# A planner's due times: later query and key products, and naturals placed within six tenths of a unit

## The chip, the cores and the metric

The kernel runs on one core of one Trainium2 chip. The metric is the time on the device in microseconds (us). Every engine of the core (TensorE or PE, VectorE or DVE, ScalarE or ACT, GpSimd or POOL, and SP, which only issues transfers) works through a queue of its own in order and meets the others at semaphores.

## What is computed

```python
x  = L0_attn_x                                   # (2, 1024, 256), float32
xn = layernorm(x)
q, k, v = (einsum('btc,hcd->bhtd', xn, W) + b)   # 16 heads of 16
probs = softmax(q @ k.T * 16**-0.5 + causal)
attn  = (probs @ v) reshaped @ Wo + bo
logits = xn @ Wr ; two best of 8 experts per row, softmax over the two
ffn = sum over e: w_e * ((clip(silu(xn @ Wg[e]), -7, 7) * (xn @ Wu[e])) @ Wd[e])
out = x + attn + ffn
```

## The kernel before

The order of everything is set before the kernel is built. `make_plan` declares jobs with an engine, a length, what they come after and a due time; `Planner.run` then lays them out one by one: of all jobs that are open it takes the one that can start soonest, and among equals the one with the earliest due time. A PSUM bank is a resource in this, with at most three naturals, three scores and two query or key products in banks at once (`ROOM`), and TensorE jobs of another kind than the last have their due time put 8000 ns later (`STAY`), since changes of kind have a price (`SWITCH`). What comes out is one list of stages for each engine, and each engine's block walks its list. The planner's lengths are its own; the chip only gets the order.

The stages, by name in the code and line in the profile:

- **Products.** `qk1` and `qk2` (L1140) are the two halves of one of 16 products of 512 rows with query or key weights; `hi` (L820) and `mid` (L826) on ScalarE, `resid` (L921) on VectorE and `lo` (L746) on POOL split each into three bfloat16 parts; SP stores a pair (`store`, L650) and loads them as packed rows (`load`, L663) for a unit. ScalarE's `hi` waits for the landing of the store two pairs back. Products 0 to 3 and 4 to 7 are the first batch row (units 0, 1 and units 2, 3). `v` (L1164) makes values and router logits for 128 rows.
- **Attention** goes in eight units of four heads. Of a unit there are first the **naturals** (`nat`, L1209): 48 chunks of scores with rows on partitions, 16 early and 32 late, whose row maxima VectorE takes (`max`, L949 on the diagonal, L952 elsewhere). `negate` (L961 to L969) turns them into bfloat16 parts, TensorE transposes these (`neg`, L1215), VectorE copies (L976), and SP writes the rows into the packed queries (L673). Then come the **scores** in 12 steps (`s`, L1228), which contain the maximum already, the exponential on ScalarE (`exp`, L848), a mask on POOL on the diagonal (L786), and the weighing of v (`pv`, L1247). Unit 0 has two such copies: neg 0 (early maxima, for steps 0 to 3) and neg 1 (for steps 4 to 11). `y_t` (L1255), `norm` (L982, L987), `proj_t` (L1264) and `proj` (L1273) close a unit.
- **Router and experts.** VectorE finds the two best experts (`top`, L1014, `topi`, L1020), makes one-hot tables (`hot`, L1031), places rows (L1037 to L1054) and builds row tables (`rows`, L1060) and digit tables (`tiles`, L1067 to L1070); TensorE counts (`route`, L1172 to L1179) and writes the lists (`list`, L1190). Only then can POOL gather rows (L760) and fetch weights (L772) for 39 tiles of 128 rows; a tile is a transpose (L1280), gate and up (L1290), tanh (L876) and hid (L1107, L1110), down (L1299), and a scatter (L778). The row tables lie in the memory of the attention's output `y`, so the first `norm` comes behind the list. The results are summed with the projection at the end (L997, L999, L1008).

The due times that matter here: attention's steps are spread from 60 to 425 us (`due_at`), a unit's naturals over the first `SPREAD` of the unit ahead of it (`nat_due`), and products 4 to 15 from 15 us on, 1.5 us apart.

Of the kernel before, what the change touches and what calls it, by code (L numbers as in the profile page):

```python
# [48 lines left out]
UNITS = B * G  # L49
# [12 lines left out]
NS = len(STEPS)  # L62
# [173 lines left out]
          ("c", "b"): 110, ("c", "f"): 120}  # L236
STAY = 8000
NEG_LAG = 8000
SPREAD = 0.75
RATE = 280  # L240
SMALL = 65536
WARM = 60
# [3 lines left out]
def make_plan():  # L246
# [3 lines left out]
    def pe(stage, ns, after=(), due=0, takes=None, mode="f", lag=None):  # L250
# [5 lines left out]
    due_at = [a0 + (a1 - a0) * (u * sum(weight) + sum(weight[:n])) / (UNITS * sum(weight))  # L256
              for u in range(UNITS) for n in range(NS)] + [a1]
    nat_weight = [chunk_width(m) + 150 for m in range(NCH)]

    def nat_due(u, m):  # L260
        if u == 0:
            return 5000 if m < EARLY else 30000 + 400 * (m - EARLY)
        begin, end = due_at[NS * (u - 1)], due_at[NS * u]
        return begin + (end - begin) * SPREAD * sum(nat_weight[:m]) / sum(nat_weight)

    for n, (ns, due) in enumerate(((1100, -30), (2000, 30), (1800, 31))):
# [13 lines left out]
    for k in range(QKS):  # L280
        b, grp, op, n = qk_tile(k)
        w = k // 2
        due = 10 * n + 6 + op if k < 4 else 15000 + 1500 * (k - 4)
        after = [("ACT", ("xnt", 2 * b + n, c)) for c in range(DC)] + [("ACT", ("weights",))]
        pe(("qk1", k), 853, after, due=due, takes=("qk", k))
        pe(("qk2", k), 853, [("PE", ("qk1", k))], due=due - 1)
        job("ACT", ("hi", k), 570, [("PE", ("qk2", k))] + ([("SP", ("store", w - 2))] if w >= 2 else []), due=due)
        job("DVE", ("resid", k), 662, [("ACT", ("hi", k))] + ([("POOL", ("lo", k - 2))] if k >= 2 else []), due=due,
            frees=("qk", k))
        job("ACT", ("mid", k), 524, [("DVE", ("resid", k))], due=due)  # L290
        job("POOL", ("lo", k), 1175, [("ACT", ("mid", k))], due=due)
        if op:
            job("SP", ("store", w), 1500, [("POOL", ("lo", k))], due=due, lag=2000, size=786432)

    for t in range(NT):
        due = 10000 + 600 * t
        pe(("v", t), 884, [("ACT", ("xnt", t // 4, c)) for c in range(DC)] + ([("DVE", ("v_ones",))] if t == 0 else []),
           due=due, takes=("v", t))
# [26 lines left out]
    for u in range(UNITS):  # L325
        b, g = divmod(u, G)
        for c in range(2):
# [3 lines left out]
            due = 8 + 10 * c if u == 0 else 60000 + c if u == 1 else nat_due(u, 0) - 30000 + c  # L331
# [3 lines left out]
    for u in range(UNITS):  # L335
        for m in range(NCH):
            width, due = chunk_width(m), nat_due(u, m)
# [3 lines left out]
    for x, (u, c0, c1) in enumerate(NEGS):  # L341
        due = nat_due(u, 0)
# [6 lines left out]
    for g in range(NS * UNITS):  # L349
        u, n = divmod(g, NS)  # L350
        c, j = STEPS[n]
        due, width = due_at[g], step_span(n)[1]
# [14 lines left out]
        if last_of_half(n):  # L367
            due = due_at[g + 1]
# [20 lines left out]
    for i in range(MAX_TILES):  # L389
        due = m0 + (m1 - m0) * i / MAX_TILES  # L390
# [965 lines left out]
```

How the kernel before makes its waits and increments, by code:

```python
        def wait_room(pe, stage):  # L597
            bank, n = FILL_AT[stage]
            if n:
                pe.wait_ge(freed[bank], n)
            return bank, filled[bank]
# [1 line left out]
        def wait_filled(eng, stage):  # L604
            bank, n = FILL_AT[stage]
            eng.wait_ge(filled[bank], n + 1)
            return bank
# [1 line left out]
        def wait_freed(eng, stage):  # L609
            bank, n = FILL_AT[stage]
            eng.wait_ge(freed[bank], n + 1)
# [1 line left out]
        def wait_weighed(eng, g):  # L614
            u, n = divmod(g, NS)
            if last_of_half(n):
                wait_filled(eng, ("y", u, STEPS[n][0]))
            else:
                eng.wait_ge(pv_done, pv_counted(g))
# [17 lines left out]
            def spread_ones():  # L638
                sp.wait_ge(consts, 2)
                sp.dma_start(packk[MAXROW:KROWS, :, :, :, :].rearrange("p s c h t -> p (s c h t)")
                             .rearrange("p (r t) -> p r t", t=T),
                             ones_row[MAXROW:KROWS, :].unsqueeze(1).to_broadcast([PARTS, SLOTS * UH, T])).then_inc(ones_in, 16)
# [1 line left out]
            def store(w):  # L644
                b, grp, _, n = qk_tile(2 * w)
                sp.wait_ge(qk_lo, 2 * w + 2)
                for part in range(PARTS):
                    cols = slice(T * b + BANK * n, T * b + BANK * (n + 1))
                    sp.dma_start(qk_d[:, grp, part, :, :, cols].rearrange("o d h t -> (d h) o t"),
                                 stage[:, w % 2, part, :].rearrange("p (o t) -> p o t", o=2)).then_inc(qk_out[w % 2], 16)
```

## Time and profile before

| | us |
|---|---|
| median of three runs (lowest, highest) | 471.8 (470.96, 472.11) |
| the profiled execution, its own time | 466.59 |
| its span, first to last instruction | 464.8 |
| TensorE busy / VectorE busy / ScalarE busy | 429.5 / 313.4 / 243.8 |
| mean granted TensorE clock, of full speed | 0.978 |

The span and every row below are of the profiled execution. A clock of 1.00 in a stretch is 2.4 GHz throughout; the lower level is 1.2 GHz, so 0.75 is half of the stretch at either. TensorE's matmuls are pipelined and their ends are modelled, so starts are the better measure. A wait is the idle time of an engine ahead of an instruction, named by who released it.

### The profile page before, as it was taken

What the parts mean: (1) busy time and instruction counts of PE and PEld (TensorE: products, weight loads), DVE (VectorE), ACT (ScalarE), POOL (GpSimd) and SP (SyncE); (2) the same over time, 40 slices, a digit from 0 to 9 for tenths busy, and PEclk for the clock granted to TensorE, in tenths of its full rate; (3) what the DMA queues carried; (4) which work ended last, traced back from release to release, by engine and by line L of the source; (5) the groups of instructions that cost most, each with busy time, mean ns of one, the idle gap of its engine ahead of it and who ended that gap; (6) DMA issues with size and microseconds to landing.
All of it is one profiled execution on the core that took longest, in us unless ns stands there. A gap on an engine that the chain in (4) does not pass through costs nothing.

```text
span 464.8 us, 8495 instructions
## 1 busy us (share of the span) xinstructions
PE 429.5 (92%) x2851; PEld 253.5 (55%) x2851; DVE 313.4 (67%) x1007; ACT 243.8 (52%) x607; POOL 196.3 (42%) x239
## 2 busy tenths in 40 slices
PE   7999969479989999999999979999999999999985
PEld 7585423133563465556575656566564665557434
DVE  4917797998987847756747555765767665672593
ACT  1564355026438646644645536655566554655862
POOL 5411225141353375456843554246633654324211
PEclk9999979968999999999999999999999999999999
DMA  8089884236392269353944388144955444400691
GB/s 277 13 211 261 240 219 135 69 118 246 66 190 77 80 161 252 97 176 104 253 169 148 102 212 243 37 147 135 249 153 168 115 171 132 128 21 21 203 298 45
DMA packets 40374, 71.35 MB, mean 154 GB/s; under 512 B 5893, under 2 KB 30598, under 8 KB 40332
## 3 DMA queue, kind: packets, MB, share of 16 engines
q0 software_dynamic: 9360, 39.99, 26.9%
q1 hardware_dynamic: 27996, 27.54, 24.3%
q10 hardware_dynamic: 2976, 3.29, 2.2%
q8 instruction: 23, 0.38, 0.4%
q14 instruction: 19, 0.16, 0.1%
HBM read 55.85 MB, written 15.60 MB: 154 GB/s over the span
## 4 chain that ended last, share of the span: by engine, by line
PE 74%; DVE 7%; DMA 6%; ACT 5%; issue 4%; POOL 2%; SPq 1%; another core or an unknown queue 0%; ACTq 0%; POOLq 0%
PE psum L1247 14%; PE psum L1290 14%; PE psum L1228 13%; PE psum L1209 12%; PE psum L1299 8%; PE psum L1140 4%; DMA qk_parts<-stage 3%; ACT probs L848 3%; PE psum L1273 3%; DVE psum L949 2%; PE psum L1164 2%; PE psum L1280 2%; DMA x<-in_x 2%; DVE mxa L952 2%; PE psum L1255 1%
## 5 line engine op out<-in xcount | busy, mean ns | idle before, releaser
L848 ACT ACTIVATE probs<-psum 128x512 f32<-128x512 f32 (+3 forms) x384 | 158.6, 508 | 60.8 <-PE psum L1228 54.8
L949 DVE CUSTOM_DVE_ANT_0 psum<-psum,maskrow 128x128 f32<-128x128 f32 (+3 forms) x256 | 122.2, 505 | 30.7 <-PE psum L1209 27.5
L1228 PE MATMUL psum<-packq,packk 99*128 99x512 bf16 (+3 forms) x384 | 98.3, 335 | 4.7 <-ACT probs L848 3.1
L1209 PE MATMUL psum<-packk,packq 96*128 96x512 bf16 (+3 forms) x384 | 96.5, 334 | 4.4 <-ACT probs L848 1.6
L952 DVE TENSOR_REDUCE mxa<-psum 128x1 f32<-128x512 f32 x128 | 87.8, 686 | 11.6 <-PE psum L1209 11.2
L1247 PE MATMUL psum<-probs,v 128*32 128x512 f32 (+3 forms) x768 | 77.5, 495 | 3.9 <-POOL probs L786 3.2
L786 POOL TENSOR_SCALAR_AFFINE_SELECT probs<-probs 128x512 f32<-128x512 f32 x64 | 41.2, 647 | 78.1 <-ACT probs L848 76.2
L1209 PEld LDWEIGHTS psum<-packk,packq 96*128 96x128 bf16 x384 | 35.5, 99 | 55.4 <-issue 18.6
L1228 PEld LDWEIGHTS psum<-packq,packk 99*128 99x128 bf16 x384 | 35.0, 98 | 52.2 <-issue 18.0
L760 POOL DMA_INDIRECT xg<-xn_rows,token x39 | 37.7, 967 | 34.4 <-PE psum L1280 27.3
L1107 DVE SCALAR_TENSOR_TENSOR tanh<-tanh,psum 128x256 f32<-128x256 f32 x39 | 16.4, 420 | 49.9 <-ACT tanh L876 40.8
L778 POOL DMA_INDIRECT expert_rows<-yo,slots x39 | 39.4, 1011 | 23.4 <-issue 12.6
L1290 PEld LDWEIGHTS psum<-xgt,wexp 128*128 128x128 f32 x384 | 45.2, 192 | 3.9 <-issue 3.4
L1290 PE MATMUL psum<-xgt,wexp 128*128 128x128 f32 x384 | 46.9, 276 | 0.0
L876 ACT ACTIVATE tanh<-psum 128x256 f32<-128x256 f32 x39 | 15.0, 384 | 60.4 <-PE psum L1290 56.1
L772 POOL DMA_INDIRECT wexp<-in_wexp,wrow x24 | 23.2, 968 | 54.4 <-PE psum L1299 37.5
L746 POOL TENSOR_TENSOR stage<-resid,stage 128x512 bf16<-128x512 f32 x16 | 19.8, 1254 | 30.7 <-ACT stage L826 30.6
L1140 PE MATMUL psum<-xnt,wqk 128*128 128x512 f32 x64 | 32.1, 626 | 0.7 <-DVE resid L921 0.7
L1247 PEld LDWEIGHTS psum<-probs,v 128*32 128x32 f32 x768 | 17.2, 108 | 27.9 <-issue 20.5
L882 ACT ACTIVATE yo<-psum 128x256 f32<-128x256 f32 x39 | 15.0, 386 | 28.7 <-PE psum L1299 27.8
L1290 PEld LDWEIGHTS psum<-xgt,xnt 128*128 128x128 f32 x240 | 28.8, 192 | 1.6 <-issue 1.1
L1290 PE MATMUL psum<-xgt,xnt 128*128 128x128 f32 x240 | 29.5, 276 | 0.0
(121 smaller groups left out, 470.2 us busy)
## 6 DMA issues: line engine op xcount, KB each, us to landing
qk_parts<-stage SPq DMA_DIRECT2D x24, 256.0 KB, 3.2
stage<-expert_rows SPq DMA_DIRECT2D x16, 256.0 KB, 4.0
packq<-qk_parts SPq DMA_DIRECT2D x16, 192.0 KB
packk<-qk_parts SPq DMA_DIRECT2D x16, 192.0 KB
x<-in_x SPq DMA_DIRECT2D x4, 512.0 KB, 8.6
packq<-qk_parts SPq DMA_DIRECT2D x16, 128.0 KB
packk<-qk_parts SPq DMA_DIRECT2D x16, 128.0 KB
xn_rows<-probs ACTq DMA_DIRECT2D x4, 512.0 KB, 12.9
```

Of the source, the lines that this page charges most:

```text
L760: pool.indirect_dma_start(out=xg[:, i % 2, :], out_offset=None, in_=xn_d, in_offset=bass.IndirectOffsetOnAxis(ap=token[:, i:i + 1], axis=0))\
L778: pool.indirect_dma_start(out=z_d, out_offset=bass.IndirectOffsetOnAxis(ap=slots[:, i:i + 1], axis=0), in_=yo[:, i % 2, :], in_offset=None ...
L786: pool.affine_select(out=cols, in_=cols, compare_op=ALU.is_ge, fill=0.0, base=0, pattern=[[0, UH], [1, P]], channel_multiplier=-1).then_in ...
L848: act.activation(probs[:, g % RING, h, 0:width], psum[:, bank, 0:width], ACT.Exp, scale=SCALE)\
L949: ins = dve.tensor_tensor_reduce(out=chunk, in0=chunk, in1=maskrow[:, BANK - width:], scale=1.0, scalar=NEG, op0=ALU.add, op1=ALU.max, acc ...
L952: ins = dve.tensor_reduce(into, chunk, op=ALU.max, axis=AX.X)
L1140: return pe.matmul(psum[:, bank, :], wqk[:, op, c, P * grp:P * (grp + 1)], xnt_moe[:, c, cols], start=c == 0, stop=c == DC - 1)
L1209: pe.matmul(psum[:, bank, 0:width], packq[0:MAXROW, u % SLOTS, i // HALF, h, P * (i % HALF):P * (i % HALF + 1)], packk[0:MAXROW, u % SLOTS ...
L1228: pe.matmul(psum[:, bank, 0:width], packk[0:KROWS, u % SLOTS, j // HALF, h, P * (j % HALF):P * (j % HALF + 1)], packq[0:KROWS, u % SLOTS, ...
L1247: ins = pe.matmul(psum[32 * h:32 * h + 32, bank, t0 - BANK * c:BANK], v[:, TB * b + j, at:at + 32], probs[:, g % RING, h, 0:width], start= ...
L1290: ins = pe.matmul(psum[:, bank, P * m:P * (m + 1)], wexp[i % WSLOTS][:, at:at + P], xgt[:, i % 2, c, :], start=c == 0, stop=c == DC - 1)
L1299: ins = pe.matmul(psum[:, bank, 0:D], hid[:, i % 2, P * c:P * (c + 1)], wexp[i % WSLOTS][:, at:at + D], start=c == 0, stop=c == DC - 1)
```

## The change

Three numbers of the plan change: the due time of products 4 to 15, `SPREAD`, and, for the last unit alone, the time in which its naturals are due, which lies 10 us sooner.

```diff
--- before.py
+++ after.py
@@ -236,7 +236,7 @@
           ("c", "b"): 110, ("c", "f"): 120}
 STAY = 8000
 NEG_LAG = 8000
-SPREAD = 0.75
+SPREAD = 0.6
 RATE = 280
 SMALL = 65536
 WARM = 60
@@ -260,7 +260,8 @@
     def nat_due(u, m):
         if u == 0:
             return 5000 if m < EARLY else 30000 + 400 * (m - EARLY)
-        begin, end = due_at[NS * (u - 1)], due_at[NS * u]
+        ahead = 10000 * (u == UNITS - 1)
+        begin, end = due_at[NS * (u - 1)] - ahead, due_at[NS * u] - ahead
         return begin + (end - begin) * SPREAD * sum(nat_weight[:m]) / sum(nat_weight)
 
     for n, (ns, due) in enumerate(((1100, -30), (2000, 30), (1800, 31))):
@@ -280,7 +281,7 @@
     for k in range(QKS):
         b, grp, op, n = qk_tile(k)
         w = k // 2
-        due = 10 * n + 6 + op if k < 4 else 15000 + 1500 * (k - 4)
+        due = 10 * n + 6 + op if k < 4 else 35000 + 1500 * (k - 4)
         after = [("ACT", ("xnt", 2 * b + n, c)) for c in range(DC)] + [("ACT", ("weights",))]
         pe(("qk1", k), 853, after, due=due, takes=("qk", k))
         pe(("qk2", k), 853, [("PE", ("qk1", k))], due=due - 1)
```

Everything else in the order follows from the planner. The lengths of all lists of stages stay the same. On VectorE, at the copy of neg 1 (L976 before, L977 after; line numbers behind the change are one higher), the engine that is waited for there. `mxa` and `mxb` are row maxima, `negm` and `negr` their negated parts, `y` and `wexp` hold the router's tables, `topi` the indices of the best experts. Before:

```order
L949 ISA psum,mxa<-psum,maskrow 128x128
L949 ISA mxa 128x1
L961 TENSOR_TENSOR mxa<-mxa,mxb 128x16
L966 TENSOR_SCALAR negm<-mxa 128x16
L967 SCALAR_TENSOR_TENSOR negr<-mxa,negm 128x16
L968 CAST negm<-negr 128x16
L969 TENSOR_TENSOR negm<-negr,negm 128x16
L1060 TENSOR_TENSOR y<-iota_row,posrow 128x2048
L976 COPY negt<-psum 96x128
L1067 TENSOR_TENSOR wexp<-iota_t,postile 128x16x39
L1069 TENSOR_TENSOR wexp<-wexp,high_digit 128x16x39
```

The copy stands behind the second row table and in front of the second digit table. After:

```order
L922 SCALAR_TENSOR_TENSOR resid<-psum,bqk,stage 128x512
L962 TENSOR_TENSOR mxa<-mxa,mxb 128x16
L967 TENSOR_SCALAR negm<-mxa 128x16
L968 SCALAR_TENSOR_TENSOR negr<-mxa,negm 128x16
L969 CAST negm<-negr 128x16
L970 TENSOR_TENSOR negm<-negr,negm 128x16
L950 ISA psum,mxa<-psum,maskrow 128x128
L950 ISA mxa 128x1
L1021 MAX_INDEX topi<-top,lg 128x8 x16
L1022 TENSOR_TENSOR dl<-top 128x16
L977 COPY negt<-psum 96x128
```

The copy now stands ahead of both pairs of tables, of placing and of the one-hot table, with the residual of product 9 just ahead of the negation, and the index search in front of it.

On TensorE, ahead of the lists (L1190, L1191), the engine that waits there; `packk,packq` are naturals, `packq,packk` scores, `probs,v` the weighing, `ident,yraw` a transposition. Before:

```order
L1209 MATMUL psum<-packk,packq 128x256
L1209 MATMUL psum<-packk,packq 128x512
L1209 MATMUL psum<-packk,packq 128x384
L1209 MATMUL psum<-packk,packq 128x512 x2
L1209 MATMUL psum<-packk,packq 128x128
L1209 MATMUL psum<-packk,packq 128x256
L1209 MATMUL psum<-packk,packq 128x384
L1209 MATMUL psum<-packk,packq 128x512
L1215 MATMUL psum<-identb,negm 96x128
L1209 MATMUL psum<-packk,packq 128x128
L1190 MATMUL psum<-wexp,y 128x78 x32
```

Only naturals, of units 0 and 1, stand between the first transposition of the output and the lists. After:

```order
L1229 MATMUL psum<-packq,packk 128x128 x3
L1229 MATMUL psum<-packq,packk 128x512 x3
L1248 MATMUL psum<-probs,v 32x256 x4
L1229 MATMUL psum<-packq,packk 128x512
L1248 MATMUL psum<-probs,v 32x128 x4
L1229 MATMUL psum<-packq,packk 128x512 x2
L1256 MATMUL psum<-ident,yraw 128x128 x4
L1229 MATMUL psum<-packq,packk 128x512 x6
L1248 MATMUL psum<-probs,v 32x512 x12
L1229 MATMUL psum<-packq,packk 128x512
L1191 MATMUL psum<-wexp,y 128x78 x32
```

In this place stand unit 0's scores of steps 3 to 7 and their weighing of v; no natural is among them. The naturals of unit 1 from the ninth on come behind the lists.

Counted over the whole list, TensorE changes its kind of matmul 239 times before and 273 times after, 56 and 95 of them ahead of unit 1's first scores. Ahead of those stand, before, three gate and up products, two down products, three row transposes and 18 naturals of unit 2; after, six, four, six and 24. Unit 7's last 32 naturals stand within 26.0 us of TensorE work before and 19.0 after (each stage at its duration in the trace).

## Rows read from the trace of the kernel before

**Rows 1.** The page: busy time of TensorE and VectorE, chain by engine, weighing of v
```profile
PE 429.5 (92%) x2851; PEld 253.5 (55%) x2851; DVE 313.4 (67%) x1007; ACT 243.8 (52%) x607; POOL 196.3 (42%) x239
...
PE 74%; DVE 7%; DMA 6%; ACT 5%; issue 4%; POOL 2%; SPq 1%; another core or an unknown queue 0%; ACTq 0%; POOLq 0%
...
L1247 PE MATMUL psum<-probs,v 128*32 128x512 f32 (+3 forms) x768 | 77.5, 495 | 3.9 <-POOL probs L786 3.2
```

**Rows 2.** Busy by stretch; columns as the first line names them
```profile
core 0: us, PE busy (x) PEld busy (x) DVE busy (x) ACT busy (x) POOL busy (x), PEclk, DMA share, GB/s
46.00:137.00 91.00, 74.29 (x420) 35.02 (x421) 78.93 (x277) 35.83 (x78) 30.41 (x31) 0.89 0.60 160
46.00:60.00 14.00, 11.67 (x33) 5.07 (x33) 10.92 (x72) 4.43 (x9) 4.59 (x4) 1.00 0.89 239
80.00:95.00 15.00, 6.53 (x49) 3.04 (x50) 14.52 (x42) 2.32 (x8) 3.50 (x4) 0.86 0.20 64
95.00:110.00 15.00, 13.80 (x77) 5.89 (x74) 13.46 (x51) 6.73 (x12) 6.87 (x7) 0.68 0.65 214
137.00:428.00 291.00, 283.77 (x2022) 173.33 (x2020) 187.06 (x590) 165.04 (x418) 143.79 (x167) 1.00 0.49 144
428.00:465.00 37.00, 30.21 (x211) 15.02 (x211) 20.22 (x46) 22.66 (x59) 6.36 (x9) 1.00 0.53 171
```

**Rows 3.** The chain that ended last: start us, us, what
```profile
26.88 5.34 PE psum L1164 x24
...
90.31 2.28 DVE y L1060
...
99.58 0.59 DVE psum L949
...
124.33 5.50 DMA xg<-xn_rows,token
...
133.68 1.79 PE psum L1290 x16
```

**Rows 4.** Timeline of VectorE: start us, us, engine, line, operation
```profile
46.82 0.21 DVE L976 COPY negt<-psum 96x128 bf16<-96x128 bf16 x1
...
48.16 0.09 DVE L1020 MATCH_VALUE_LOAD topi<-top,lg 128x8 f32 x1
...
50.47 0.75 DVE L921 SCALAR_TENSOR_TENSOR resid<-psum,bqk,stage 128x512 f32<-128x512 f32 x1
...
61.67 0.28 DVE L1037 TENSOR_TENSOR fits<-psum,iota 128x128 f32<-128x128 f32 x1
...
64.54 1.41 DVE L921 SCALAR_TENSOR_TENSOR resid<-psum,bqk,stage 128x512 f32<-128x512 f32 x2
...
85.11 0.69 DVE L952 TENSOR_REDUCE mxa<-psum 128x1 f32<-128x512 f32 x1
...
89.14 0.33 DVE L949 CUSTOM_DVE_ANT_0 psum<-psum,maskrow 128x128 f32<-128x128 f32 x1
...
92.52 0.21 DVE L976 COPY negt<-psum 96x128 bf16<-96x128 bf16 x1
...
92.65 0.80 DVE L1067 TENSOR_TENSOR wexp<-iota_t,postile 128x624 bf16<-128x624 f32 x1
...
94.50 0.43 DVE L949 CUSTOM_DVE_ANT_0 psum<-psum,maskrow 128x256 f32<-128x256 f32 x1
```

**Rows 5.** Timeline of TensorE, three places
```profile
36.44 0.76 PE L1209 MATMUL psum<-packk,packq 96*128 96x128 bf16 x5
...
94.69 2.24 PE L1190 MATMUL psum<-wexp,y 128*128 128x78 bf16 x32 [3.93 <-issue]
...
136.99 1.03 PE L1228 MATMUL psum<-packq,packk 99*128 99x512 bf16 x4
```

**Rows 6.** Timelines of SP's queue and ScalarE
```profile
43.06 1.46 SPq L650 DMA_DIRECT2D qk_parts<-stage  x3
...
54.08 0.69 ACT L820 ACTIVATE stage<-psum,bqk 128x512 bf16<-128x512 f32 x1 [3.31 <-DMA qk_parts<-stage]
...
56.78 3.94 SPq L650 DMA_DIRECT2D qk_parts<-stage  x6
...
62.70 1.27 ACT L820 ACTIVATE stage<-psum,bqk 128x512 bf16<-128x512 f32 x2 [4.68 <-DMA qk_parts<-stage]
...
92.75 1.77 SPq L673 DMA_DIRECT2D packq<-negt  x3
```

## The prediction

> **What bounds the kernel now.** I read the page's first table and its chain of waits first. TensorE (PE) is busy 92% of the span and carries 74% of the chain that ended last; VectorE (DVE) stands at 67% [rows 1]. So the end moves when TensorE's idle time, or its time at the lower clock, changes: the change leaves every matmul in place. Next I read the table by stretch, to see where those two lie. From 137 to 428 us TensorE is busy 283.8 of 291 us at full clock, 7.2 us idle. From 428 on it is idle about 6.6 us of 36.8, in the drain of the last unit. But from 46 to 137 us it is idle 91 - 74.3 = 16.7 us, at a mean granted clock of 0.89, so about 20 us of that stretch ran at 1.2 instead of 2.4 GHz [rows 2]. This early stretch is the pool from which the change can gain. Within it, from 80 to 95 us, TensorE works 6.5 of 15 us while VectorE works 14.5: VectorE is the engine that ends last there.
>
> The chain of waits says the same: from 84 to 100 us it runs over VectorE (row maxima, then the one-hot tables of the router), and later over one gather of expert rows [rows 3]. In order of time, VectorE copies the first unit's early maxima at 46.8 us (neg 0), then does the whole top-two search, residuals and router tables; it finishes unit 0's later maxima, 32 chunks, only at about 89.4 us and copies neg 1 at 92.5, after the first half of the router's second table [rows 4]. The scores of the second half of unit 0 need that copy on its way through SP (issued 92.75), so they start near 100 us; the routing list is on TensorE at 94.7; unit 1's first scores run at 137.0 [rows 5, 6]. TensorE had nothing else: its queue is in order, and what stands there is unit 1's naturals, which wait for VectorE.
>
> **The change part by part.** No operation is added or taken out, so the direct price is zero; all of it is order.
>
> (1) Query and key products 4 to 15 come later. Until 36 us nothing starves: v products fill the place (5.34 us for six [rows 3], 0.89 each, which the copy on ScalarE keeps up with), and naturals begin near 36.4 us as now [rows 5]. Unit 0's naturals now run straight through: in the order, all 48 stand ahead of product 10. The two stores to DRAM that these products feed come later on SP, behind neg 0, and with them unit 2's loads; unit 2's naturals stand far behind the lists, so this is hidden. What it costs if that cover is gone: the next products wait for the landing of a store two pairs back. Rows show 11.0 us for one (issued 43.06, released ScalarE at 54.08), among heavy traffic, and 5.9 us for the next (56.78 to 62.70); I take 6, since the loads that crowded the queue at 43 us are gone by then, and keep 11 in the range [rows 6].
>
> (2) VectorE from 46.8 us. A head of eight late chunks takes 85.11 to 89.14 = 4.03 us, four heads 16.1 [rows 4]. In the new order, behind the copy of neg 0, there stand about 31 of these chunks (15.6 us), six residuals at 0.67 (0.75 less the overlap, 4.0), the negation (0.9: from the last chunk at 89.14 to the table at 90.31 [rows 3], less 0.25 for the chunk), one small chunk (0.2) and the index search (48.16 to 50.47 = 2.3). Sum 23.1: neg 1 is copied at 46.8 + 23.1 = **70 us instead of 92.5**. TensorE keeps up with that: up to neg 1 it has 12.2 (before its first real work) + 48.6 us of matmuls, 61 us, and waits about 8 for VectorE.
>
> (3) Then the router on VectorE: six residuals (4.0), seven small steps at 0.3 (2.1), four diagonal chunks (4.03 less four others at 0.6, which is 0.69 less the overlap: 1.6), placing (61.67 to 64.54 = 2.9), two row tables at 2.2 (4.4), two digit tables at 1.85 (92.65 to 94.50; 3.7). Sum 18.7, ready at 88.7 us. TensorE has 18.8 us of matmuls from neg 1 to the list: last products 6.9, weighing of v for seven steps 5.7 (0.81 each in the mean [rows 1]), scores 4.0, the rest 2.2; with 2 us of changes of kind (some 0.1 each), 70 + 21 = 91. The list, 2.2 us [rows 5], ends at **93 us, against 96.9**: the router itself gains 4 us at most. The gain is that scores and v of six and a half steps lie ahead of it, where TensorE stood idle.
>
> (4) From the list to neg 2: TensorE 22.5 us of matmuls (scores and v of steps 7 to 11, 40 naturals, four gate/up products) plus 2.7 us of changes; VectorE 1 + 40 chunks (19.7) + 1.4 + 1.2 = 23.3. The last four chunks are ahead of neg 2 on both, and naturals run at most three ahead of VectorE, so I add 2.5 for the coupling: 93 + 27.7 = 120.7. From there to unit 1's first scores 10.8 us of matmuls: 131.7. The experts' inputs: gather 2 stands on POOL behind the mask of step 11 in both orders and took 5.5 us to land [rows 3]; now it is issued near 108, lands near 114, and is wanted at 115. No gain, no loss; if late, up to 2 us.
>
> (5) The clock. My walk is at full clock. TensorE has pauses in 47 to 57 and again near 70 us, so it will lose some; before, about 10 us of half clock fell where TensorE was the bound (95 to 110: 0.68 [rows 2]). I take 2 us: **133.7 us against 137.0**, 3.3 sooner. And more is done by then: ahead of unit 1's first scores the new order has three more gate/up products (3 x 1.79 [rows 3]), two down products (1.7), three transposes (0.7) and six late naturals (1.1), 8.9 us. So TensorE is 3.3 + 8.9 = **12.2 us ahead**.
>
> (6) SPREAD and the last unit. From there on both orders hold the same work but 8.9 us less, with 5 fewer changes of kind (the planner's own price, 0.1 each; 0.5). Naturals come denser: of unit 7 the last 32 lie within 19.0 us of TensorE work and need 18.7 on VectorE, where now it is 26.0 to 19.7. That is the tightest place; -1 to +3 us, taken as +0.5. In the drain, the first eight heads' projection now stands ahead of step 6's scores, so ScalarE rests there and has four more exponentials behind it (2 us) while TensorE has 0.9 less ahead: even, 0 to 1.
>
> Sum: 464.8 - 12.2 = 452.6 us of span, 454.4 for the profiled execution (466.6 before, with 1.8 around the span). The median of the runs is 471.8, 5.2 above that execution; the difference is taken from it: **471.8 - 12.3 = 459.5 us**.
>
> **The rivals.** (A) *The gain is given back* in 137 to 428 us. Being ahead is worth something only while TensorE is the bound there. For: denser naturals make VectorE and TensorE wait for one another in units 5 to 7; 1.5 us for each of six units gives back 9. Against: idle 7.2 of 291 us [rows 2]. Time 468. By the Trainium skill, "Trainium Kernel Development and Optimization", Performance Expectations, matmul busy time says little of how near TensorE is to its limit and weight-load time says more; the page shows 55% for the latter. That rule would make this rival likely; the short waits in 137 to 428 speak against it.
>
> (B) *Only the router counts*: the experts' chain (39 tiles) sets the end, and it starts 4 us sooner: 468. Against: the end is paced by a full TensorE, and POOL, which issues their transfers, is little in the chain (2%) [rows 1]. A and B end alike.
>
> (C) *Slower: the clock.* In 47 to 57 us the order leaves TensorE small naturals with gaps, in place of long products. If the clock falls there and stays low until the list and beyond, each microsecond of bound TensorE work costs one more. Up to neg 2 some 43 us of work are concerned; from 14.2 us of it on, the gain is gone; 20 us give 471.8 - 14.2 + 20 = 477.6. For: after 92 us the clock stayed low for much of 15 us though TensorE was busy 13.8 of them [rows 2]. Against: in 46 to 60 it stayed full with 2.3 us idle. The Trainium skill, "TensorE: Matmul & The Clock Gate", section "Why this matters for your kernels", has it that pauses between bursts bring the throttle, which speaks against this order of short bursts; the trace agrees as far as the drops begin behind waits.
>
> (D) *It does nothing*: a store's landing (11 us, [rows 6]) holds products 12 to 15 and so the router, 6 us late, and the clock takes the rest: within 0.3%, 471.8.
>
> (E) *More*: no clock loss and tighter coupling, gain 18 to 20: 452.5.
>
> **How the numbers follow.** A measurement can tell about 0.3%, 1.4 us. Forecast (454 to 464) 0.58; A and B (464 to 470.3) 0.17; E 0.05; D 0.07; C 0.13. Faster 0.80, same 0.07, slower 0.13. The range takes in E's edge and A and B: 452.5 to 470.
>
> **What would show it.** Neg 1's copy near 70 and its SP issue at 70 to 72 us; VectorE busy nearly throughout 47 to 89; TensorE's list near 91; idle from 46 us to unit 1's first scores down from 16.7 to about 9, with those scores near 134; mean clock there 0.9 or more; some 8 us idle from there to the last down product. Wrong if: the clock is under 0.8 in 50 to 120 (C), ScalarE waits over 6 us for a store (D), or TensorE's idle time behind unit 1's first scores grows by more than 5 us (A).

## The result, and the profile after

The changed kernel runs in 467.98 us (median of 20 runs) beside 470.69 us for the kernel before on the same chip: 0.9941 of its time, 95% interval 0.9915 to 0.9968. That is faster by 0.6%, or 2.7 us, where 12.3 us was forecast: the sign is right, the size is not. The time lies inside the stated range (452.5 to 470), but outside the band given the most weight (454 to 464). Measured twice more, the ratio was 0.9979 (0.9949 to 1.0009) and 0.9993 (0.9957 to 1.0029); the mean of the three is 0.997, by which the gain is about 1.3 us (an estimate over three chips).

The profiled execution of the changed kernel took 467.66 us, its span is 465.9. That of before (466.59) lies under all 20 runs that the kernel before has beside the changed one (468.49 at the lowest), so the ends of the two traces say little.

The page after, for [rows 1]: busy times, chain by engine, weighing of v.

```profile
PE 434.4 (93%) x2851; PEld 257.6 (55%) x2851; DVE 315.0 (68%) x1007; ACT 243.8 (52%) x607; POOL 195.0 (42%) x239
...
PE 71%; DVE 16%; ACT 4%; DMA 3%; issue 3%; POOL 2%; another core or an unknown queue 1%; POOLq 0%; SPq 0%; DVEq 0%; ACTq 0%
...
L1248 PE MATMUL psum<-probs,v 128*32 128x512 f32 (+3 forms) x768 | 76.9, 496 | 4.6 <-POOL probs L787 3.9
```

The chain now runs over VectorE for 16% of the span (7% before). The table by stretch after, for [rows 2]; columns are the stretch, its length, busy us (and count) of PE, PEld, DVE, ACT, POOL, the granted clock, DMA share, GB/s.

```profile
46.00:137.00 91.00, 79.95 (x460) 39.84 (x461) 83.93 (x270) 40.43 (x87) 36.22 (x38) 0.94 0.60 168
46.00:60.00 14.00, 11.83 (x35) 4.76 (x36) 13.73 (x43) 3.23 (x5) 3.18 (x3) 0.88 0.34 110
80.00:95.00 15.00, 13.52 (x77) 4.86 (x79) 14.27 (x19) 11.00 (x26) 6.61 (x6) 0.95 0.32 106
95.00:110.00 15.00, 13.96 (x106) 4.88 (x98) 13.72 (x51) 8.00 (x19) 8.79 (x10) 1.00 0.61 214
120.00:130.00 10.00, 7.14 (x47) 6.56 (x47) 6.62 (x27) 1.30 (x4) 1.89 (x2) 0.83 0.25 61
137.00:428.00 291.00, 281.61 (x1972) 170.86 (x1970) 182.89 (x585) 160.61 (x408) 138.06 (x162) 0.99 0.49 140
```

Before, TensorE stood idle for long in one place. That hole is gone: from 80 to 95 us TensorE is busy 13.5 of 15 us, not 6.5, and from 95 to 110 it has the full clock, not 0.68. Two things are new. From 120 to 130 us there is a smaller hole with the clock at 0.83, and from 137 to 428 us TensorE is idle 9.4 us instead of 7.2, its clock no longer full.

The milestones, for [rows 4, 5]: VectorE's copy of neg 1, TensorE's list, and unit 1's first scores.

```profile
71.44 0.22 DVE L977 COPY negt<-psum 96x128 bf16<-96x128 bf16 x1
...
95.93 1.23 PE L1191 MATMUL psum<-wexp,y 128*128 128x78 bf16 x29
...
140.48 1.03 PE L1229 MATMUL psum<-packq,packk 99*128 99x512 bf16 x4
```

Neg 1 was forecast for 70 (92.5 before) and came at 71.4. The list was forecast for 91 and came at 95.9; neg 2 for 120.7, and came at 128.7; unit 1's scores for 133.7, and came at 140.5. With the 8.9 us of work moved ahead of them, TensorE is 8.9 - (140.5 - 137.0) = 5.4 us ahead there, not 12.2. The first scores of units 4 and 6, after and before:

```profile
270.73 1.04 PE L1229 MATMUL psum<-packq,packk 99*128 99x512 bf16 x4
378.97 0.38 PE L1229 MATMUL psum<-packq,packk 99*128 99x512 bf16 x1
```
```profile
280.49 0.81 PE L1228 MATMUL psum<-packq,packk 99*128 99x512 bf16 x3
377.90 1.03 PE L1228 MATMUL psum<-packq,packk 99*128 99x512 bf16 x4
```

The two orders have different amounts of work ahead of these places: at unit 4 the new one has 4.3 us less done, at unit 6 1.6 us more (estimates, each matmul at its usual spacing in the traces). So the lead is 9.8 - 4.3 = 5.5 us at unit 4, as at unit 1, and 1.6 - 1.1 = 0.5 us at unit 6. At unit 7's first scores (428.5 for 426.5) it is -1.9. Of the 7.4 us lost between units 4 and 7 about 3.4 are the lower clock (0.98 in the mean over 270.7 to 428.5, for 1.00) and 3.0 more idle time of TensorE (5.7 us there, 2.7 before).

**Where the list is late.** VectorE's router steps became slower. Its timeline after; the first number is the start, the second the duration.

```profile
67.58 1.02 DVE L968 SCALAR_TENSOR_TENSOR negr<-mxa,negm 128x16 f32<-128x16 f32 x1
...
87.27 1.07 DVE L1068 TENSOR_TENSOR wexp<-iota_t,postile 128x624 bf16<-128x624 f32 x1
88.38 1.65 DVE L1070 TENSOR_TENSOR wexp<-wexp,high_digit 128x624 bf16<-128x624 bf16 x1
89.94 1.28 DVE L1071 TENSOR_SCALAR wexp<-wexp,low_digit 128x624 bf16<-128x624 bf16 x1
...
93.34 0.80 DVE L1068 TENSOR_TENSOR wexp<-iota_t,postile 128x624 bf16<-128x624 f32 x1
94.18 0.81 DVE L1070 TENSOR_TENSOR wexp<-wexp,high_digit 128x624 bf16<-128x624 bf16 x1
94.90 0.39 DVE L1071 TENSOR_SCALAR wexp<-wexp,low_digit 128x624 bf16<-128x624 bf16 x1
```

The same three steps of a digit table take 4.0 us at 87 and 2.0 us at 93. What differs is GpSimd, which splits the products' third parts (`lo`) at just these times:

```profile
66.15 2.41 POOL L747 TENSOR_TENSOR stage<-resid,stage 128x512 bf16<-128x512 f32 x2 [0.67 <-ACT stage L827]
...
87.65 3.39 POOL L747 TENSOR_TENSOR stage<-resid,stage 128x512 bf16<-128x512 f32 x2
```

From 66 to 92 us, VectorE's instructions beside such a subtraction take 5.7 us more than their like without one, 1.4 of it ahead of neg 1 and 4.3 behind it; in before it is about 1.1 us, two instructions at 75 and 76 us, since there only two subtractions lay beside router steps. By the Trainium skill, "SBUF — State Buffer", section "Who interferes with whom", GpSimd and VectorE have a port pair in common that one of them holds for a whole instruction; the durations agree with that.

**Where neg 2 is late.** TensorE's timeline, with the wait ahead of an instruction in brackets:

```profile
119.72 0.38 PE L1281 MATMUL psum<-ident,xg 128*128 128x128 f32 x2
119.98 0.22 PE L1210 MATMUL psum<-packk,packq 96*128 96x128 bf16 x1
123.05 0.69 PE L1281 MATMUL psum<-ident,xg 128*128 128x128 f32 x2 [2.86 <-DMA xg<-xn_rows,token]
123.53 0.42 PE L1210 MATMUL psum<-packk,packq 96*128 96x256 bf16 x1
123.75 3.00 PE L1291 MATMUL psum<-xgt,wexp 128*128 128x128 f32 x16
```

The rows of tile 3 are not there. Their gather needs one of two buffers of `xg`, which the transposes of tile 1 free; on GpSimd, gathers 2 and 3:

```profile
112.28 0.95 POOL L761 DMA_INDIRECT xg<-xn_rows,token  x1 [0.99 <-PE psum L1281]
116.61 0.95 POOL L761 DMA_INDIRECT xg<-xn_rows,token  x1 [3.38 <-PE psum L1281]
```

The gather for tile 3 is issued at 116.6, and its rows are used at 123.1. Behind the wait the clock has fallen: 16 matmuls of gate and up take 3.00 us where they take 1.95 to 2.02 around it.

### The profile page after: what moved, and what is told of

Same layout as the page of the kernel before. It is cut to its first block, busy times and chain, and to the rows that moved or that the text cites. A ratio compares the mean times of both kernels' runs of the same rounds, so it can differ in the third digit from the quotient of the medians.

```text
span 465.9 us, 8495 instructions
## 1 busy us (share of the span) xinstructions
PE 434.4 (93%) x2851; PEld 257.6 (55%) x2851; DVE 315.0 (68%) x1007; ACT 243.8 (52%) x607; POOL 195.0 (42%) x239
## 3 DMA queue, kind: packets, MB, share of 16 engines
q1 hardware_dynamic: 27996, 27.54, 23.9%
## 4 chain that ended last, share of the span: by engine, by line
PE 71%; DVE 16%; ACT 4%; DMA 3%; issue 3%; POOL 2%; another core or an unknown queue 1%; POOLq 0%; SPq 0%; DVEq 0%; ACTq 0%
PE psum L1291 15%; PE psum L1248 13%; PE psum L1210 12%; PE psum L1229 10%; PE psum L1300 7%; DVE psum L950 5%; ACT probs L849 4%; PE psum L1274 3%; PE psum L1141 3%; DVE mxa L953 3%; PE psum L1165 3%; PE psum L1281 2%; DMA x<-in_x 2%; PE psum L1256 2%; DMA xg<-xn_rows,token 1%
## 5 line engine op out<-in xcount | busy, mean ns | idle before, releaser
L849 ACT ACTIVATE probs<-psum 128x512 f32<-128x512 f32 (+3 forms) x384 | 159.1, 513 | 50.6 <-PE psum L1229 48.0
L1229 PE MATMUL psum<-packq,packk 99*128 99x512 bf16 (+3 forms) x384 | 96.2, 329 | 4.5 <-issue 1.4
L953 DVE TENSOR_REDUCE mxa<-psum 128x1 f32<-128x512 f32 x128 | 87.9, 687 | 13.9 <-PE psum L1210 12.9
L1210 PEld LDWEIGHTS psum<-packk,packq 96*128 96x128 bf16 x384 | 35.3, 97 | 57.5 <-issue 23.1
L1291 PEld LDWEIGHTS psum<-xgt,wexp 128*128 128x128 f32 x384 | 48.4, 200 | 3.3 <-issue 2.1
L1291 PE MATMUL psum<-xgt,wexp 128*128 128x128 f32 x384 | 49.3, 284 | 0.3 <-DVE mxa L953 0.2
L1248 PEld LDWEIGHTS psum<-probs,v 128*32 128x32 f32 x768 | 18.4, 108 | 32.6 <-issue 22.8
L1141 PE MATMUL psum<-xnt,wqk 128*128 128x512 f32 x64 | 33.9, 645 | 1.1 <-DVE negt L977 0.7
```

Source lines behind the costliest of these rows:

```text
L849: act.activation(probs[:, g % RING, h, 0:width], psum[:, bank, 0:width], ACT.Exp, scale=SCALE)\
L953: ins = dve.tensor_reduce(into, chunk, op=ALU.max, axis=AX.X)
L1141: return pe.matmul(psum[:, bank, :], wqk[:, op, c, P * grp:P * (grp + 1)], xnt_moe[:, c, cols], start=c == 0, stop=c == DC - 1)
L1210: pe.matmul(psum[:, bank, 0:width], packq[0:MAXROW, u % SLOTS, i // HALF, h, P * (i % HALF):P * (i % HALF + 1)], packk[0:MAXROW, u % SLOTS ...
L1229: pe.matmul(psum[:, bank, 0:width], packk[0:KROWS, u % SLOTS, j // HALF, h, P * (j % HALF):P * (j % HALF + 1)], packq[0:KROWS, u % SLOTS, ...
L1248: ins = pe.matmul(psum[32 * h:32 * h + 32, bank, t0 - BANK * c:BANK], v[:, TB * b + j, at:at + 32], probs[:, g % RING, h, 0:width], start= ...
```

## The experiments

All ratios are to the kernel before on the same chip, with 95% intervals. The chips differ: before took 461.3 us on two of them and 468 to 471 on the others, so kernels are compared within a group of runs on one chip. Each kernel of this part was timed 12 times, but five of those with a third buffer only 6 times; their intervals are wider.

### Each edit alone

These four ran on one chip. **The kernel before again.** 

> The kernel before, unchanged, as a second trace and as a measure of what a repeat differs by. Every theory: ratio 1.000 within 0.003, some 470.7 us. If the profiled execution of before (466.6 us) was merely a quick one, this trace has the expert stage or the last unit some 2 to 4 us later than the first one had, with the same stages up to unit 1's first scores (near 137 us).

Measured: 1.0015 (0.9988 to 1.0042). In time this is 462.1 us, not 470.7: this chip is a faster one. Its trace has unit 1's first scores at 138.2, and is ahead of the first trace only from unit 4 on (first scores at 278.2 for 280.5, unit 6 at 374.2 for 377.9).

**Products alone**, one line:

```diff
-        due = 10 * n + 6 + op if k < 4 else 15000 + 1500 * (k - 4)
+        due = 10 * n + 6 + op if k < 4 else 35000 + 1500 * (k - 4)
```

> Only the due time of the products 4 to 15 is moved (35000 for 15000), the naturals keep 0.75 and the last unit's their place. Theory S (the products bring all of the gain, and it is carried to the end): the same as the changed kernel or better, ratio 0.990 to 0.995, 466 to 468 us. Theory G (the denser naturals give back in the units 4 to 6 what the start won, a lead of 5.4 us at unit 4's scores and 0.2 at unit 6's in the first pair of traces): without them the full 5.4 us is kept, ratio 0.988 to 0.990, some 465.3 us, 2 us and more below the changed kernel. Theory N (the naturals are what brings the gain): ratio 0.998 to 1.002, about 470.7 us.

Measured: 0.9963 (0.9937 to 0.9989), 1.7 us. This is clear of 1.000, but in no theory's range: the interval reaches into those of S and N, and G's (the full 5.4 us kept) falls. In its trace the list comes at 97.5 and unit 1's first scores at 144.4, behind waits for gathered rows (1.7 and 4.4 us) and half the clock from 125 on: the lead of the list is lost before unit 1.

**Spread alone** (`SPREAD = 0.6`). 

> Only the spread of the naturals goes from 0.75 to 0.6. The prediction priced this at about nothing: ratio 0.998 to 1.002. Theory G (denser naturals cost time in the units 4 to 6): 1.003 to 1.008, 472 to 474 us. Theory N (they bring the gain): 0.994 to 0.997, about 468.5 us.

Measured: 1.0061 (1.0024 to 1.0097), a cost of 2.8 us, as theory G expected. The forecast had it at about nothing. The profiled execution does not show that cost as a whole: its time is 462.8 us, for 463.9 of the kernel before on this chip.

**The last unit alone** (the two lines with `ahead`). 

> Only the last unit's naturals come 10 us of the plan's time sooner. The prediction gave this 0.5 us at the most: ratio 0.998 to 1.001. If it is the last unit's earlier naturals that crowd the units 5 and 6, 1.003 to 1.006 (472 to 473.5 us), with unit 6's first scores later than in before and the tail of unit 7 shorter by less.

Measured: 0.9989 (0.9954 to 1.0023), no difference that the interval can tell.

### What holds the start up

These four ran on one chip. **The changed kernel again.** 

> The changed kernel, unchanged, for a second trace and a second ratio against before. First ratio 0.994 (0.992 to 0.997). Every theory: 0.992 to 0.997. If the lead over before of 5.4 us at unit 4's first scores and 0.2 us at unit 6's, seen in the first pair of traces, is a property of the order (theory G), this trace shows again half a clock or idle time of TensorE between 300 and 380 us; if it was that one execution, this one keeps some 3 us of it or more.

Measured: 0.9979 (0.9949 to 1.0009), a little above the range of every theory. The second question is answered in part. Against the trace of before on the other fast chip the lead falls again, from 4.9 us at unit 4's first scores (269.0 for 278.2) to 2.1 at unit 6's (373.6 for 374.2) and -0.8 at unit 7's, which speaks for the order and against one odd execution; but between 300 and 380 us this trace has the full clock. At the start, the wait for tile 3's rows is larger here, and a smaller one stands before it:

```profile
120.32 0.44 PE L1281 MATMUL psum<-ident,xg 128*128 128x128 f32 x2 [0.89 <-DMA xg<-xn_rows,token]
120.59 0.22 PE L1210 MATMUL psum<-packk,packq 96*128 96x128 bf16 x1
125.26 0.69 PE L1281 MATMUL psum<-ident,xg 128*128 128x128 f32 x2 [4.44 <-DMA xg<-xn_rows,token]
125.74 0.42 PE L1210 MATMUL psum<-packk,packq 96*128 96x256 bf16 x1
125.95 3.62 PE L1291 MATMUL psum<-xgt,wexp 128*128 128x128 f32 x16
```

**Short subtractions on GpSimd**, in the changed kernel and in before. The kernel leaves out the third parts of 496 of 512 columns, and GpSimd sets their place to zero at the start (not shown here):

```diff
-                pool.tensor_tensor(stage[:, w % 2, stored(k, 2), cols], resid[:, k % 2, :], stage[:, w % 2, stored(k, 1), cols],
+                cols = slice(BANK * op, BANK * op + 16)
+                pool.tensor_tensor(stage[:, w % 2, stored(k, 2), cols], resid[:, k % 2, 0:16], stage[:, w % 2, stored(k, 1), cols],
```

> The changed kernel with GpSimd's subtraction for the third parts of queries and keys on 16 of the 512 columns (the other third parts are left at zero, so scores lose their last digits). Theory P (GpSimd's subtractions of 1.2 us each hold up VectorE's router steps, 5.7 us in the changed kernel's trace): the router's steps are back at their durations without a neighbour (hot 0.49 us and not 1.8), the token list 4 to 5 us sooner than in the changed kernel (91 to 92 us for 95.9), and the ratio to before 3 to 4 us lower than the changed kernel's, about 0.986 to 0.988. Theory Q (the list is late for another reason, the copies of ScalarE or a store): list within 1.5 us of 95.9, ratio 0.992 to 0.996.

> The same cut of GpSimd's subtractions in the kernel before, as the control. Theory P: two of them lie beside the router there, about 1 us of VectorE, and TensorE waits for negated maxima, not for the list: 0.997 to 1.000. If GpSimd's subtractions cost as much here as in the changed kernel (they hold up the chunk maxima or the stores as well), 0.990 to 0.993, and the cut tells nothing about the change.

Measured: the changed kernel 0.9988 (0.9952 to 1.0024), before 0.9964 (0.9934 to 0.9995). VectorE's slow steps are nearly gone (a digit table takes 2.0 us both times, the one-hot table 0.8 for 1.8), yet the changed kernel is no faster; before is, by 1.4 us, which is just below theory P's range for it and not in the other's. Two things in the trace of the changed kernel go with that. At the start, ScalarE's queue stands for 4.9 us at 36.8, in the issue of a store that takes 0.7 us in the changed kernel, and neg 1 comes at 74.5, 2.3 us later; that the zeros set by GpSimd cause this is not shown. The list comes 0.8 us later, so 1.5 us are won back up to there. And neg 2 stands at 132.1, with 132.2 in the changed kernel: TensorE's wait for the gathers takes up what was won. Theory P's mechanism held on VectorE; its price at the end did not. The test was not clean, and was made again below.

**A third buffer for gathered rows**, the order unchanged. The space is that of the query and key weights:

```diff
-        xg = sb("xg", [P, 2, D])
+        xg_own = sb("xg", [P, 2, D])
+        xg = [xg_own[:, 0, :], xg_own[:, 1, :], wqk[:, 0, 0, :]]
...
-                if i >= 2:
-                    wait_filled(pool, ("x", i - 2))
+                if i == 2:
+                    wait_filled(pool, ("qk", QKS - 1))
+                if i >= 3:
+                    wait_filled(pool, ("x", i - 3))
```

> The changed kernel with a third buffer for gathered rows (in the space of the query and key weights, free by then), so that gather 2 does not wait for the transposes of tile 0, nor gather 3 for those of tile 1. Everything is computed. Theory X (the gathers' chain, with the 2.9 us for which TensorE waits before the transposes of tile 3 and the half clock behind it, costs 3 to 4 us ahead of unit 1's first scores): no wait there, those scores at 136.5 to 138 us for 140.5, ratio to before 3 us lower than the changed kernel's, about 0.987. Theory Y (the wait only takes the place of one for neg 2, which VectorE could not have given sooner): scores of unit 1 within 1 us of 140.5, ratio 0.993 to 0.996.

Measured: 0.9893 (0.9847 to 0.9939), by the medians 4.6 us below before and 4.1 below the changed kernel on that chip. In its trace:

```profile
120.45 0.44 PE L1284 MATMUL psum<-ident,xg 128*128 128x128 f32 x2 [0.88 <-DMA xg<-xn_rows,token]
120.84 1.95 PE L1294 MATMUL psum<-xgt,wexp 128*128 128x128 f32 x16
123.01 1.95 PE L1294 MATMUL psum<-xgt,xnt 128*128 128x128 f32 x16
124.79 0.22 PE L1219 MATMUL psum<-identb,negm 128*96 128x128 bf16 x1
```

Tile 3 waits 0.9 us, not 4.4, the matmuls behind it have the full clock, neg 2 stands at 124.8 for 132.2, and unit 1's first scores at 136.2 for 143.3. Theory X holds; Y falls. Later traces agree: with the products moved and whole subtractions, unit 1's first scores stand at 140.5 to 144.4 us in the five traces with two buffers, and at 136.2 to 140.1 in the seven with three.

### Is it the change that needs the buffer?

Four more, on one chip. **Before with the third buffer.** 

> The kernel before with the third buffer for gathered rows; everything is computed. In its trace only one gather's wait shows on TensorE, 1.67 us at 129.88, and 1.7 us are all that can be won. Theory X1 (it is the change that puts the gathers on the path: work moved behind the list runs out before the rows come): 0.996 to 1.000 here, against the 0.989 of the changed kernel with the third buffer. Theory X2 (a third buffer is worth as much in either order, and the last run's gain says nothing on the change): 0.989 to 0.993.

Measured: 1.0035 (1.0000 to 1.0071), no gain; rather slower than X1's range. The wait of 1.67 us is gone from the trace, unit 1's first scores come 0.5 us sooner, and no gain is left at the end. X2 falls, and X1 is what remains: only the changed order gains from the buffer.

**Products alone, third buffer.** 

> Only the products' due time of the change, with the third buffer. Theory S (the products bring all of the gain; denser naturals and the last unit's lead bring nothing with the gathers free either): as the changed kernel with the third buffer, 0.987 to 0.992. If the denser naturals are what pays once the gathers do not hold TensorE up, 0.993 to 0.996. If they cost what they cost alone (1.006), 0.983 to 0.986 and the best kernel so far.

Measured: 0.9834 (0.9787 to 0.9882), 459.9 us for 467.8. This is what was expected if the denser naturals cost here what they cost alone, and the lowest ratio up to here.

**Short subtractions and third buffer**, the edit above from the fifth product on, so that the start stays. 

> The changed kernel with the third buffer, and GpSimd's subtraction for the third parts on 16 of 512 columns from the fifth product on (the first four whole, so that the start is as in the changed kernel; the other third parts keep what the first four left, so scores differ in their last digits). Theory P (5.7 us of VectorE's time beside those subtractions puts the list late, and with the gathers free that goes to the end): the list at 92 to 93 us for 95.8, unit 1's first scores at 133 us for 136.2, ratio 0.980 to 0.983. Theory R (VectorE ends 0.5 us before TensorE comes to the list; TensorE's own queue sets it): the list 1 to 2.5 us sooner at the most, ratio 0.985 to 0.989.

**The changed kernel with the third buffer, again.** 

> The changed kernel with the third buffer once more, since half of its runs were left out the first time. Every theory: 0.989 within 0.004, 4 to 6 us below before; its trace has unit 1's first scores at 136 to 137 us.

Measured: 0.9897 (0.9838 to 0.9956) with the short subtractions beside 0.9953 (0.9907 to 0.9998) without. The last is above the 0.985 to 0.993 that every theory expected, while its trace has unit 1's first scores where they were expected (136.4). Products alone is 7.5 us below it (459.9 for 467.4): what differs is the spread and the last unit. With the short subtractions the list stands at 92.0 for 95.6, unit 1's first scores at 134.6 for 136.4, the medians at 464.1 for 467.4. The ratio is above the ranges of both theories, its interval reaching into R's, and the two intervals overlap, so the 3.3 us at the end is a hint. The 3.6 us at the list is what theory P named; how they get there is more of theory R:

```profile
89.06 0.39 DVE L1076 TENSOR_SCALAR wexp<-wexp,low_digit 128x624 bf16<-128x624 bf16 x1
...
92.01 1.34 PE L1196 MATMUL psum<-wexp,y 128*128 128x78 bf16 x32
```

VectorE's last table is ready at 89.4, 5.5 us sooner, and 2.6 us ahead of the list, which stands where TensorE's own queue comes to it. Of the 3.6 us 1.8 are left at unit 1; between 115 and 125 us the granted clock is 0.83 there, a loss of 1.7 us, and 1.00 without the short subtractions.

### What the denser naturals cost

Four, on one chip, all with the third buffer: the two by two of the spread and the last unit.

> Products' due time and third buffer, once more, as the base of the two by two. Theory G (naturals give back): 0.983 to 0.987, the fastest of these four. Theory V (all four are equal, the earlier differences were of chips and runs): 0.988 to 0.992 for all four.

> The same with the spread at 0.6, the last unit's naturals where they were. Theory G, denser naturals are the cost (0.6% alone): 0.989 to 0.993, 3 us above the base. Theory V: as the base within 0.3%.

> The same with the spread at 0.75 and the last unit's naturals 10 us of the plan sooner. Alone that edit measured 0.999. Theory G by the spread: as the base within 0.3%, or 0.1% better. If it is the last unit's part that costs beside the moved products, 0.988 to 0.993.

> The changed kernel with the third buffer, all three edits, a third time (0.989 and 0.995 so far). Theory G: 0.990 to 0.995, 3 to 4 us above the base. Theory V: as the base within 0.3%.

| products moved, third buffer, and | runs | us | ratio (95%) |
|---|---|---|---|
| nothing else | 6 | 462.8 | 0.9813 (0.9768 to 0.9858) |
| spread 0.6 | 12 | 469.6 | 0.9994 (0.9961 to 1.0026) |
| last unit | 6 | 460.0 | 0.9776 (0.9735 to 0.9817) |
| both (the whole change) | 12 | 469.2 | 0.9954 (0.9921 to 0.9987) |

The spread takes 1.8% in the ratios, 6.8 us by the medians, nearly everything the products win (8.4 us); with the last unit's naturals sooner it takes 1.8% again, 9.1 us (460.0 to 469.2). Theory G names the direction; the cost is two to three times its 3 to 4 us. V falls. The last unit's edit costs nothing and may bring 0.4%; the intervals overlap. The kernel with the products moved, the last unit's naturals sooner and the third buffer, at the old spread, beats both: 0.9776, 11 us below before.

Why it costs, as far as the traces show. Two 20-us stretches at the end of unit 5's scores, first at spread 0.75, then at 0.6 (columns as above):

```profile
340.00:360.00 20.00, 19.92 (x129) 11.88 (x128) 13.79 (x40) 11.49 (x25) 7.94 (x9) 1.00 0.37 122
360.00:380.00 20.00, 19.43 (x154) 12.40 (x153) 11.52 (x43) 9.67 (x27) 12.40 (x15) 1.00 0.49 160
```
```profile
340.00:360.00 20.00, 19.34 (x121) 10.09 (x120) 16.61 (x51) 11.06 (x25) 6.78 (x8) 1.00 0.38 133
360.00:380.00 20.00, 17.88 (x119) 12.77 (x121) 5.44 (x19) 8.27 (x25) 10.31 (x12) 0.83 0.35 116
```

At 0.6 VectorE has more to do first (16.6 of 20 us), then almost nothing (5.4): most naturals are done, and TensorE has few left to put between the scores (6 of their matmuls from 360 to 380 us, for 15). It then stands still for short times, and what follows runs at half clock:

```profile
369.19 0.28 PE L1231 MATMUL psum<-packq,packk 99*128 99x128 bf16 x2 [0.53 <-issue]
...
370.77 0.38 PE L1231 MATMUL psum<-packq,packk 99*128 99x512 bf16 x1 [0.64 <-issue]
371.96 1.46 PE L1231 MATMUL psum<-packq,packk 99*128 99x512 bf16 x3 [0.82 <-ACT probs L851]
```

From unit 5's first scores to unit 6's it takes 50.6 us (320.2 to 370.8), against 46.0 (325.3 to 371.3) at 0.75; TensorE is idle 3.8 us of that, against 0.7, and has some 1 us more work. The lower clock comes behind it, in unit 6.

Between 145 and 430 us, the time lost to the lower clock is 0.0 us in all ten traces at spread 0.75, and 1.7 to 5.1 us in eight of nine at 0.6 with the products moved. From 430 us on it is the other way round: seven of the ten at 0.75 lose 1.8 to 3.4 us in the drain of the last unit, all at 0.6 at most 0.7. So the clock alone does not explain the cost; the idle time from 137 to 428 us is the other part (6.8 to 7.9 us with the third buffer at 0.75, and 5.9 to 12.6 at 0.6 and the products moved; 5.9 is the one trace on a fast chip).

With the spread alone the lower clock takes nothing behind 145 us. TensorE is idle 4.0 us from 137 to 428, for 2.4 in the trace of before on that chip: 1.6 of the 2.8 us. The rest I can't place.

### The same with two buffers

Two runs, on one chip: the change without its spread, and the whole.

> The change without its spread of 0.6: the products' due time and the last unit's naturals, two buffers for gathered rows. Theory G (the spread gives back what the products win): 0.985 to 0.992, 3 us and more below the changed kernel on this chip. Theory H (the two-buffer gathers cap the gain first, so that the spread makes no difference there): within 0.3% of the changed kernel, 0.993 to 0.998.

> The changed kernel, unchanged, on the same chip: 0.994 and 0.998 so far. Both theories: 0.993 to 0.998.

Measured: 0.9958 (0.9919 to 0.9997) and 0.9993 (0.9957 to 1.0029); medians 467.8 and 469.0. The second is a little above the range expected for it. The difference, 1.3 us, is less than the intervals can tell: G and H stay open here. The two traces tell more: at unit 7's first scores the kernel without the spread is far ahead (421.8 for 429.1; 5.4 us when the work done is counted), as G has it, and then gives most of it back. It loses 3.4 us to the lower clock in the drain (0.91 from 430 to 470, for 0.99), and the spans are 465.1 and 466.8. So in this pair of traces the spread costs time in units 4 to 6 with two buffers as well, and little of it reaches the end.

## Why the prediction was right or wrong

**Step 1, the products later: right.** Naturals start at 36.8. ScalarE waited 2.7 us for a store, once, at 77; rival D named over 6 us and falls.

**Step 2, neg 1 at 70: right** (71.4). From neg 0 to neg 1 VectorE took 23.9 us for 23.1 counted, though `mxa` and `negr` were 1.4 us slower beside GpSimd; the rest of the count was 0.6 us too long.

**Step 3, the router: mis-sized.** The forecast had VectorE ready at 88.7 and TensorE's queue at the list at 91; they came at 95.3 and 95.9. The sum took VectorE's durations from places where GpSimd did nothing. In the new order GpSimd's subtractions lie beside the router, and 5.7 us of VectorE's time goes to that, against 1.1 before. With the subtractions cut (and the third buffer) VectorE is ready at 89.4 and the list comes at 92.0: about 1 us from the forecast. By which waits VectorE's delay gets into TensorE's queue was not followed.

**Step 4, list to neg 2: mis-sized.** "Gather 2 stands on POOL behind the mask of step 11 ... no gain, no loss" looked at one gather and its queue. With two buffers each gather waits for the transposes of the tile two back. In the new order tiles 0 to 3 follow one another about 4 us apart on TensorE (111.6, 116.0, 119.7, 123.1; before, tile 3 comes only at 157.2), so gather 2 is issued at 112.3 instead of 108, and gather 3, of which nothing was said, at 116.6. Together with the lower clock behind the wait, list to neg 2 took 32.8 us for the 29.7 forecast, and 35.7 in the second trace. With the third buffer it takes 29.0. With both causes taken away, unit 1's first scores stand at 134.6; the forecast was 133.7 (and 0.2 less if its last sum is added rightly: 120.7 + 10.8 is 131.5).

**Step 5, the clock: about right, and not a fixed sum.** From 40 to 145 us the granted clock is 0.90 before and 0.95 or 0.93 after, so 10 us were lost to it before and 5 to 7 after, 3 with the third buffer. Before, after, after again and with the third buffer:

```profile
40.00:145.00 105.00, 87.56 (x488) 40.78 (x487) 90.53 (x317) 46.06 (x108) 36.80 (x39) 0.90 0.62 172
```
```profile
40.00:145.00 105.00, 93.06 (x522) 46.03 (x520) 97.86 (x329) 46.95 (x103) 43.13 (x45) 0.95 0.63 183
```
```profile
40.00:145.00 105.00, 90.88 (x513) 45.87 (x510) 95.16 (x320) 44.49 (x96) 40.99 (x41) 0.93 0.63 177
```
```profile
40.00:145.00 105.00, 95.12 (x563) 46.03 (x562) 99.51 (x332) 50.16 (x114) 45.94 (x49) 0.97 0.64 185
```

The forecast took 2 us for it and set them behind everything else. In the trace 5.1 are lost, in three dips of 1.7, near 51, 78 and 123 us. The first lies where TensorE waits for VectorE anyway; only the third lies behind the wait for the gathers, on the way to neg 2. Neg 2 came 8.0 us late (4.9 at the list, 3.1 from there on) and unit 1's scores 6.8: none of the clock's loss fell between the two, where the sum had put it. With the products alone, 10 us were lost again. TensorE's idle time from 46 to 137 us fell from 16.7 to 11.1 us; 9 was forecast. Rival C falls, since the dips are short and the mean clock is 0.94 from 46 to 137 us; so does B, since the list is later than before (95.9 for 94.7) and the 5.4 us ahead at unit 1 are work done; and so does E.

**Step 6, the spread: wrong.** It was taken at +0.5 us, by looking at the last unit alone. Alone it costs 2.8 us, and beside the moved products with the gathers free 6.8. With two buffers, as in the changed kernel, the times put it at 1.3 us and cannot tell that from nothing, though the traces lose their lead in units 4 to 6. This is rival A, in its place (units 5 to 7) and near its time (468); but only about half of the missing gain went its way, and the rest was lost ahead of unit 1, so that the time agrees is in part luck. A's own sign, over 5 us more idle time behind unit 1's first scores, did not show either: it was 2.2 us more (9.4 for 7.2), with 3.4 us of lower clock beside it, which A left out. A was argued against from the 7.2 us of idle time in 137 to 428 us of before. That argument failed: idle time there was short with the naturals mixed into the scores as they were, and says nothing of an order that puts them first. The last unit's edit was rightly priced (0 to 0.4% gain).

So of the 12.2 us ahead that were forecast, 6.8 were lost up to unit 1's first scores by steps 3 and 4, and the 5.4 left were lost in units 4 to 6, where the order of step 6 has the naturals early.

The kernel with the products moved, the last unit's naturals sooner and a third buffer gains 11.1 us, near the 12.3 of the forecast. That too is in part luck: its list comes at 96.2 and unit 1's first scores at 138.0, 5.2 and 4.3 us behind the forecast, like those of the changed kernel. In the changed kernel the gathers cap the gain at the start, and the spread takes what the buffer would give. The two do not add: by the medians the buffer with the spread kept gains 0.4 to 4.6 us on before (three chips), two buffers without the spread 3.1.

## What to carry to other kernels

- When a reorder brings the consumers of a ring of buffers closer together, walk the ring: for each transfer ask which instruction frees its buffer, and when that one now runs. The change made two buffers too few where a third had gained nothing.
- Take the duration of a VectorE instruction from a place where GpSimd does what it will do beside it, not from the quietest place.
- Measure each number of a tuned table by itself. Here one of three edits won, one was neutral, and one gave the win back: independent work spread between steps that wait was worth more than the same work done early.

## What the runs showed of the hardware

- VectorE's slow steps all have their tensors in SBUF and stretch to about the end of a neighbouring GpSimd subtraction: `negr` on 16 columns takes 1.02 us beside one of 1.2 us and 0.17 without. A `resid` step, which reads PSUM too, takes 0.75 us beside one (65.94) and 0.74 without (52.59).
- The clock can fall without one long pause just ahead of it: in the changed kernel it falls near 51 us (0.51 from 50.8 to 54.2). The last pause over 1 us ends at 46.8; from 46.9 to 50.8 TensorE is busy 2.7 of 3.9 us, with waits of 0.15 to 0.32.
- The rows of a gather (128 rows) are used 6.4 us after its issue in one trace of the changed kernel and 9.1 us in another (116.61 to 123.05, 116.16 to 125.26), TensorE waiting for them both times; [rows 3] has 5.5 from issue to landing.
- The same kernel on two chips (the changed one with the third buffer) stands within 0.4 us in both traces up to unit 2's first scores (166.9 and 167.3) and 13.9 us apart at the end (spans 451.9 and 465.8). Between 145 and 430 us the second has 10.5 us of TensorE pauses for 4.1, put down to exponentials, their copies and "issue", and lost 5.1 us to the lower clock for 0.0. Why one chip starts these pauses is open.
